# A recommendation-model kernel: the TensorE order around the pair products, and the output layers in three parts

## What is computed

```python
B, NF, D, V, NDENSE = (512, 26, 64, 12500, 13)      # as run
h = relu(dense @ dw1 + db1)
dense_emb = relu(h @ dw2 + db2)
sparse_emb = emb_tables[f_ids, sparse_idx]          # 512 x 26 rows of 64 floats
emb = concatenate([dense_emb[:, None, :], sparse_emb], axis=1)
inter = einsum('bfd,bgd->bfg', emb, emb)
pairs = inter[:, iu0, iu1]                          # 351 pairs
z = concatenate([emb.reshape(B, -1), pairs], axis=1)
z = relu(z @ ow1 + ob1)                             # 512 wide
z = relu(z @ ow2 + ob2)                             # 256
z = relu(z @ ow3 + ob3)                             # 128
return z @ ow4 + ob4
```

## Time and profile before

| | us |
|---|---|
| median of 3 runs | 188.66 |
| lowest and highest | 187.30, 188.84 |
| the profiled execution, its own time | 187.21 |
| its span (first to last instruction) | 185.4 |
| PE busy | 127.4 |
| POOL busy | 123.8 |
| mean granted TensorE clock | 0.88 of full |

### The profile page before, as it was taken

One profiled execution on the slowest core, in us unless ns is written; L12 is line 12 of the kernel. 1 busy time (PEld: TensorE's weight loads), 2 busy tenths in 40 slices (PEclk: granted clock), 3 DMA queues, 4 the chain that ended last, 5 costly groups with the idle time before them and its releaser, 6 DMA issues.

```text
span 185.4 us, 3069 instructions
## 1 busy us (share of the span) xinstructions
PE 127.4 (69%) x1301; PEld 68.8 (37%) x1301; DVE 37.8 (20%) x97; ACT 42.2 (23%) x96; POOL 123.8 (67%) x199
## 2 busy tenths in 40 slices
PE   1510285828655995839439993959729979989994
PEld 0000132514344442524226432424426446656453
DVE  2700003000142204100144005000234023136011
ACT  0440310031046201040075001040174011166011
POOL 3888888888735888888565888888367887200000
PEclk9999999975965699996965798587997999999999
DMA  5999532221212332312312332222222324100000
GB/s 157 409 332 357 172 26 23 23 28 21 21 13 23 21 22 24 28 22 26 24 13 24 23 27 20 23 28 20 19 20 20 22 25 31 18 4 0 4 0 0
DMA packets 4576, 9.80 MB, mean 53 GB/s; under 512 B 2065, under 2 KB 2065, under 8 KB 3922
## 3 DMA queue, kind: packets, MB, share of 16 engines
q0 software_dynamic: 3328, 3.41, 21.3%
q1 hardware_dynamic: 1010, 5.30, 7.1%
q10 hardware_dynamic: 224, 0.89, 1.6%
HBM read 9.59 MB, written 0.00 MB: 52 GB/s over the span
## 4 chain that ended last, share of the span: by engine, by line
PE 45%; POOL 26%; issue 18%; ACT 5%; DMA 3%; DVE 2%
PE acc L259 20%; POOL gathered L211 20%; PE acc L292 10%; PE inter L276 7%; POOL pace L219 6%; PE acc L310 4%; DMA gathered<-tables,rows 2%; ACT emb L386 1%; ACT emb L387 1%; PE turned L240 1%; PE acc L301 1%; ACT pairs L392 1%; DMA idx_raw<-idx 1%; ACT z L399 1%; DVE emb L466 1%
## 5 line engine op out<-in xcount | busy, mean ns | idle before, releaser
L211 POOL DMA_INDIRECT gathered<-tables,rows x104 | 98.9, 951 | 34.6 <-issue 16.9
L259 PE MATMUL acc<-w,emb 128*128 128x512 f32 x104 | 65.7, 780 | 19.4 <-issue 12.3
L259 PEld LDWEIGHTS acc<-w,emb 128*128 128x128 f32 x104 | 31.3, 315 | 46.3 <-issue 36.9
L392 ACT ACTIVATE pairs<-inter 28x96 f32<-28x96 f32 (+1 forms) x64 | 15.7, 246 | 39.8 <-PE inter L276 39.1
L219 POOL MEMSET pace<- 128x192 uint8 x90 | 24.7, 274 | 0.1
L292 PE MATMUL acc<-w,pairs 128*128 128x512 f32 x56 | 24.7, 592 | 0.0
L182 DVE COPY pairs<-inter 28x96 f32<-28x96 f32 (+1 forms) x64 | 17.0, 266 | 26.5 <-PE inter L276 25.8
L276 PE MATMUL inter<-emb 64*28 64x28 f32 x1024 | 12.6, 204 | 13.8 <-DMA gathered<-tables,rows 10.1
L240 PE MATMUL turned<-small,gathered 128*128 128x128 f32 x52 | 10.1, 317 | 13.5 <-DMA gathered<-tables,rows 13.5
L386 ACT ACTIVATE emb<-turned 128x512 f32<-128x512 f32 x8 | 8.8, 1098 | 45.7 <-issue 28.6
L465 DVE COPY emb<-turned 128x512 f32<-128x512 f32 (+1 forms) x7 | 5.5, 784 | 64.1 <-issue 49.5
(11 more groups left out here) (47 smaller groups left out, 26.3 us busy)
## 6 DMA issues: line engine op xcount, KB each, us to landing
w<-w SPq DMA_DIRECT2D x5, 1024.0 KB, 8.7
gathered<-tables,rows POOLq DMA_INDIRECT x104, 3.4
small<-small_pack ACTq DMA_DIRECT2D x1, 706.5 KB, 6.0
dense_sb<-dense_pack ACTq DMA_DIRECT2D x1, 160.5 KB
idx_raw<-idx SPq DMA_DIRECT2D x1, 39.0 KB
idx_raw<-idx SPq DMA_DIRECT2D x1, 13.0 KB, 1.9
out<-y SPq DMA_DIRECT2D x1, 2.0 KB
```

The source lines that it names most:

```text
L211: pool.indirect_dma_start(out=gathered[:, t, s, :], out_offset=None, in_=tables, in_offset=bass.IndirectOffsetOnAxis(ap=rows[:, t, s:s + 1 ...
L259: nc.tensor.matmul(acc[t][:], emb[:, tile_of(t), place(2 * c)], w[:, c, :], start=(c == 0), stop=False)
L392: last = move(lambda dst, src: nc.scalar.activation(dst, src, ACT.Copy), t, k, (0, 1))
```

## The change

Three things are moved on PE; ACT and DVE follow in their own orders. POOL's and SP's instructions are the same, but for the semaphores of the last tile's groups.

1. **The end of a tile.** Before, PE did `turn` 2, the four chunks of group 2, `turn` 3, the chunk of group 3, and then the first half-stage. Now it does `turn` 2, `turn` 3, the first two chunks of group 2, the first half-stage, `turn(t+1, 0)`, then the other two chunks of group 2 and the chunk of group 3, and only then the second half-stage.
2. **The output layers in three parts** (`PARTS`): tiles 0 and 1 together (256 columns) in tile 2; tile 2 (128 columns) with its layer 2 in tile 3 and its layers 3 and 4 beside the interactions of tile 3; tile 3 as before.
3. **The last tile has five groups**: 4, 4, 2, 2 and 1 chunks (`LAST_GROUPS`).

```diff
+LAST_GROUPS = [(0, 4), (4, 8), (8, 10), (10, 12), (12, 13)]
-EARLY = LAST * P
+PARTS = [slice(0, 2 * P), slice(2 * P, 3 * P), slice(3 * P, B)]
 ...
+def groups(t):
+    return LAST_GROUPS if t == LAST else GROUPS
 ...
-            def field_products(t, g, chunks=None):
+            def field_products(t, g, first=0, end=W_GROUP):
 ...
-                for c in range(*(chunks or GROUPS[g])):
+                c0, c1 = groups(t)[g]
+                for c in range(c0 + first, min(c0 + end, c1)):
 ...
             for t in range(TILES):
                 if t:
                     interactions(t - 1, 0)
                 turn(t, 0)
                 if t:
+                    field_products(t - 1, 2, 2)
+                    field_products(t - 1, 3)
                     interactions(t - 1, 1)
                 field_products(t, 0)
                 if t:
                     pair_product(t - 1)
                     z1_to_features(t - 1, at_once)
                 turn(t, 1)
-                if t < LAST:
+                if t == LAST:
+                    break
+                if t == LAST - 1:
+                    layer2(PARTS[0], 1, whole, (acc[0], acc[1]))
+                    field_products(t, 1, 0, 2)
+                    layer3(PARTS[0], 0, acc[3])
+                    field_products(t, 1, 2)
+                    layer4(PARTS[0], 0, acc[0])
+                else:
                     field_products(t, 1)
-                    turn(t, 2)
-                    field_products(t, 2)
-                    turn(t, 3)
-                    field_products(t, 3)
-
-            layer2(early, LAST - 1, [[(m, k) for m in range(2) for k in range(K1)]], (acc[0], acc[1]))
-            c0, c1 = GROUPS[1]
-            field_products(LAST, 1, (c0, c0 + 1))
-            layer3(early, 0, acc[2])
-            field_products(LAST, 1, (c0 + 1, c0 + 3))
+                turn(t, 2)
+                turn(t, 3)
+                field_products(t, 2, 0, 2)
+
+            layer2(PARTS[1], 2, whole, (acc[1], acc[2]))
+            field_products(LAST, 1)
             turn(LAST, 2)
-            layer4(early, 0, acc[0])
-            field_products(LAST, 1, (c0 + 3, c1))
             turn(LAST, 3)
-            c0, c1 = GROUPS[2]
+            field_products(LAST, 2)
+            turn(LAST, 4)
             interactions(LAST, 0)
-            field_products(LAST, 2, (c0, c0 + 2))
+            layer3(PARTS[1], 1, acc[1])
+            field_products(LAST, 3)
             interactions(LAST, 1)
-            field_products(LAST, 2, (c0 + 2, c1))
-            field_products(LAST, 3)
+            field_products(LAST, 4)
+            layer4(PARTS[1], 1, acc[2])
             pair_product(LAST)
             z1_to_features(LAST, Z1_STEPS)
-            layer2(late, LAST, LAYER2_STEPS, (acc[1], acc[2]))
-            layer3(late, 1, turned[1])
-            layer4(late, 1, inter[0])
+            pe.wait_ge(y_done, 2)
+            layer2(PARTS[2], LAST, LAYER2_STEPS, (acc[1], acc[2]))
+            layer3(PARTS[2], 2, turned[1])
+            layer4(PARTS[2], 2, inter[0])
```

More of the change, by code:

```diff
@@ L124, in build @@
         ones_set = sem("ones_set")
-        group_in = [[sem(f"group_in{t}_{g}") for g in range(NG)] for t in range(TILES)]
+        group_in = [[sem(f"group_in{t}_{g}") for g in range(len(groups(t)))] for t in range(TILES)]
         gathers_held = sem("gathers_held")
@@ L207, in _ @@
                     pool.wait_ge(rows_done, 1)
-                for g, (c0, c1) in enumerate(GROUPS):
+                for g, (c0, c1) in enumerate(groups(t)):
                     for s in range(2 * c0, 2 * c1):
@@ L231, in turn @@
             def turn(t, g):
-                c0, c1 = GROUPS[g]
+                c0, c1 = groups(t)[g]
                 pe.wait_ge(group_in[t][g], 2 * (c1 - c0) * 16)
@@ L241, in turn @@
                                              gathered[:, t, 2 * c:2 * c + 2, :].rearrange("p f d -> p (f d)"), ident)
-                if t == LAST and g == NG - 1:
+                if t == LAST and g == NG:
                     moved(t - 1)
@@ L248, in kept @@
             def kept(t, g):
-                pe.wait_ge(kept_dve if g % 2 else kept_act, t * 2 + g // 2 + 1)
-                if t == LAST and g == NG - 1:
-                    pe.wait_ge(kept_act, t * 2 + 3)
-            def field_products(t, g, chunks=None):
+                if g % 2 or g == NG:
+                    pe.wait_ge(kept_dve, t * 2 + g // 2 + 1)
+                if g % 2 == 0:
+                    pe.wait_ge(kept_act, t * 2 + g // 2 + 1)
+            def field_products(t, g, first=0, end=W_GROUP):
                 if t == 0:
@@ L266, in interactions @@
                         pe.wait_ge(dense_placed, 1)
-                    kept(t, 2)
-                    kept(t, 3)
+                    for g in range(2, len(groups(t))):
+                        kept(t, g)
                     if t:
@@ L326, in layer4 @@
                 nc.tensor.matmul(bank[0:1, 0:n], ow4, z3t[:, samples], start=True, stop=True).then_inc(y_mm, 1)
-            early, late = slice(0, EARLY), slice(EARLY, B)
             at_once = [(0, K1)]
+            whole = [[(m, k) for m in range(2) for k in range(K1)]]
             for t in range(TILES):
@@ L385, in keep @@
                 act.wait_ge(group_turned, t * NG + g + 1)
-                nc.scalar.activation(evens(t, g), turned_all(g), ACT.Copy)
-                nc.scalar.activation(odds(t, g), turned_odds(g), ACT.Copy).then_inc(kept_act, 1)
+                nc.scalar.activation(evens(t, g), turned_all(t, g), ACT.Copy)
+                nc.scalar.activation(odds(t, g), turned_odds(t, g), ACT.Copy).then_inc(kept_act, 1)
             def moves(t, k):
@@ L425, in _ @@
                     z1_relu(t - 1, at_once)
+                if t == LAST - 1:
+                    z2_relu(PARTS[0], 0, acc[0])
+                    z3_relu(PARTS[0], 0, acc[3])
                 if t == LAST:
-                    z2_relu(early, 0, acc[0])
-                    z3_relu(early, 0, acc[2])
+                    z2_relu(PARTS[1], 1, acc[1])
                 keep(t, 2)
-            act.wait_ge(group_turned, TILES * NG)
-            nc.scalar.activation(odds(LAST, NG - 1), inter[0][D:P, 0:P].rearrange("p (c b) -> p c b", b=P), ACT.Copy) \
+            act.wait_ge(group_turned, LAST * NG + NG + 1)
+            nc.scalar.activation(odds(LAST, NG), inter[0][D:P, 0:P].rearrange("p (c b) -> p c b", b=P), ACT.Copy) \
               .then_inc(kept_act, 1)
             moves(LAST, 0)
+            z3_relu(PARTS[1], 1, acc[1])
             moves(LAST, 1)
             z1_relu(LAST, Z1_STEPS)
-            z2_relu(late, 1, acc[1])
-            z3_relu(late, 1, turned[1])
+            z2_relu(PARTS[2], 2, acc[1])
+            z3_relu(PARTS[2], 2, turned[1])
         @block.vector
@@ L499, in _ @@
                 keep(t, 1)
+                if t == LAST - 1:
+                    z2_relu(PARTS[0], 0, acc[1])
+                    outputs(PARTS[0], 0, acc[0])
                 if t == LAST:
[L501 to L506, removed]
+                    z2_relu(PARTS[1], 1, acc[2])
+                keep(t, 3)
+            dve.wait_ge(group_turned, LAST * NG + NG + 1)
+            nc.vector.tensor_copy(evens(LAST, NG), turned_all(LAST, NG)).then_inc(kept_dve, 1)
             moves(LAST, 0)
             moves(LAST, 1)
+            outputs(PARTS[1], 1, acc[2])
             z1_features(LAST, Z1_STEPS)
-            z2_relu(late, 1, acc[2])
-            outputs(late, 1, inter[0])
+            z2_relu(PARTS[2], 2, acc[2])
+            outputs(PARTS[2], 2, inter[0])
 def lay_out(inputs):
```

23 lines of the change are left out of this document (10 added, 13 removed).

## The result

| | before | changed |
|---|---|---|
| median, us | 188.50 | 195.20 |
| lowest and highest, us | 187.30, 188.84 | 193.27, 196.36 |
| span of the profiled execution, us | 185.4 | 194.5 |

The changed kernel is slower: 1.029 times the time before, 95% interval 1.022 to 1.036. That ratio compares executions in the faster of two states that a kernel shows, of the changed kernel those of 193.27 and 194.11 us; its two others, the profiled one among them, took 196.3 and 196.4 us and lift its median to 195.20. The forecast was no change at 189.4 us, from 185.9 to 192.4; the time lies above that.

The account below looks back on a forecast made before the run. POOL was taken to set the pace up to tile 3's second held gather, PE the end. 187.21 us plus 2.9 (holds), 0 (layers) and -1.2 (tail) gave 188.9, with 0.5 added 189.4 us; range 185.9 to 192.4.

Parts of the forecast that it names:

- The hold term: POOL, gather 7 to gather 11 in tiles 1 to 3: 10.7 us each, +2.9 us in all, from -3.1 to +5.0.
- may go after the longer wait: First half-stage: its inner stall of 0.82 us may vanish, which moves little since the landing comes next.
- The mechanism of the holds: Around the half-stages: PE idles about 5 us ahead, its clock falls, and the six records behind take 4.5 us.
- the high end: Holds with all six records at 1.2 GHz: 11.4 us a pair, 34.2 us in all, +5.0 us.
- The rival with half clock at both places: Slow clock between the half-stages in all tiles and in the tail: +5.3, or 192.5 us; chance 0.31.
- The tail term: End of the last tile: last chunk turned earlier, shorter way to the pair product; -1.2 us, from -2.7 to +0.3.
- the +1.5 us: Tail: price for PE's clock falling after its new waits, taken between 0 and 3 us.
- The layers in tile 2: Layers of tiles 0 and 1 done in tile 2 fit into the room made: 0 us, from 0 to +3.
- tile 2 overfull: Layers at half clock make PE up to 3 us late at tile 2's first half-stage: 191 us and more; chance 0.06.
- The offset of 0.5 us: Added for the unchanged stretches: a third of the 1.45 us by which the timed median exceeds the profiled execution.

Follow-up runs that it names:

- changed_again: The changed kernel with no edit, run once more on another chip for a second profile; 1.031 times the time before.
- padded_12: The changed kernel with three idle 128x128 matmuls (12 records with weight loads) behind the two chunks ahead of each first half-stage; 1.022 times the time before.
- before_again: The kernel before with no edit, run once more on another chip for its time and profile; 1.001 times the time before.
- shifted_28: The changed kernel with seven idle 128x128 matmuls (28 records with weight loads) at the very start; 1.028 times the time before.
- products_before_turn3: The changed kernel with the two chunks of group 2 ahead of the transpose of group 3 instead of behind it; 1.033 times the time before.
- two_between: The changed kernel with two chunks instead of three between the half-stages and three ahead of the first; 1.004 times the time before.
- layers_only: The kernel before with only the output layers in three parts, old order around the half-stages, four groups in the last tile; 1.001 times the time before.
- holds_undone: The changed kernel with all five field products of a tile's end ahead of the first half-stage again; 0.990 times the time before.

## Why the prediction was wrong

**The hold term failed, and by its size.** The step "three times 10.7 is 32.1: +2.9 us" measured +5.1 us on the first chip, for which it was made (34.24 against 29.16), and +8.3 us on the others (34.2 against 25.9).
- The end it named, 10.7 us a pair, is right where the half-stage runs through: 10.52 and 10.62 us in tiles 1 and 3 of changed_again, 10.40 to 10.60 in padded_12. The six records took 4.35, 5.11 and 4.91 us where 4.5 stood.
- The stop in tile 1's half-stage was put at nothing: such stalls "may go after the longer wait", and "that moves little". On the first chip they came to 0.71 and 1.37 us there and the pair of tile 2 to 12.86 us, 2.2 us over 10.7. That is the whole miss of the term on that chip (34.24 - 32.1 = 2.1). In changed_again one stop of 2.59 us brings 13.06 us.
- The base depends on the chip. The kernel before has 29.16 us there and 25.9 in before_again. The earlier trace rows show a part of the difference: tile 1's first half-stage stops for 0.82 us inside (tile 0's, in the same trace, for 0.59 and 0.52), and in before_again it does not. The three timed executions on the first chip were no shorter than the profiled one, so nothing shows that these stalls were a chance of one execution. Whether they are that chip's is open. Against the other chips' base the term was 5.4 us short: 3.3 for the base, 2.6 for the stop, and 0.5 the other way, since the pairs without the stop come to 31.6 instead of 32.1.

**That leaves a part of the miss on the first chip.** The two quicker executions lie 3.9 and 4.7 us above the forecast, and the holds explain 2.2. If their last gather starts where the profiled one's does, their tails are 28.4 and 29.2 us (an estimate: spans of 191.5 and 192.3 us, less 163.1) against 27.2 before, +1.2 and +2.0 us where -1.2 stood. No profile of such an execution exists there, so the cause of this part is open.

**The mechanism of the holds was right.** PE's wait of 4.8 to 6.5 us ahead of the half-stages in changed_again, the clock at 0.50 behind it, and the chunks ending after gather 10 are all there; what the earlier trace rows showed of eight records held for six. That the +5.1 us of the first chip meet the high end I had given (+5.0) is luck: that end had three slow pairs of 11.4 us and no stop, and it was reached by 10.57, 10.81 and one pair of 12.86 with the stop. The rival with half clock at both places (192.5 us, 0.31) was the nearest case. Its 11.4 us a pair was too high: the six records ran at 0.50 nearly to their end, but the half-stage behind them had the full clock and took 1.27 instead of 1.75 us.

**The tail term, -1.2 us, measured -2.0 in changed_again, and other profiles put it nearer zero.** In changed_again the last chunk is turned at 166.50, 3.45 us after its gather starts, instead of 5.8 us: -2.4 against -2.2 expected. From turn to half-stage +0.2, from half-stage to pair product 175.09 - 167.74 = 7.35 us against 7.3, where 7.1 against 7.6 stood: the narrow end gains nothing there, because the moves lie open (0.94 us). The clock stayed at 1.00, and the +1.5 us for a fallen one did not come. But in padded_12, shifted_28, products_before_turn3 and two_between, whose tile 3 is the same, it did: the four records between the half-stages took 2.9 to 3.6 us instead of 1.99, and the tail is 26.7 to 27.0 us, only 0.2 to 0.5 under that of before_again. In padded_12, with the granted clock in the window:

```profile
167.05 3.52 PE L266 MATMUL acc<-w,emb 128*128 128x512 f32 x4
```

```profile
168.00:169.00 1.00, 1.00 (x3) 0.50 0.00 0
```

And in changed_again:

```profile
169.47 1.99 PE L266 MATMUL acc<-w,emb 128*128 128x512 f32 x4
```

PE's waits before it are nearly the same in two_between, where the clock fell (1.55, 0.33 and 0.80 us), and in changed_again, where it did not (1.53, 0.34 and 0.80). So the +1.5 us, a middle between 0 and 3, was a fair price for something that came in some profiles and not in others; what decides it is open.

**The layers in tile 2, 0 us, held.** In changed_again PE waits 6.51 us ahead of tile 2's first half-stage. The rival "tile 2 overfull" did not happen. With all five chunks ahead of it the same layers do no sure harm either: the pair of tile 3 is 8.52 us in layers_only, and in holds_undone, the same kernel up to there, 9.53.

**The offset of 0.5 us** rested on the profiled execution being quick among its neighbours. No run prices it. What the other chips add is where the chips differ: spans of 185.4 and 182.2 us, 3.2 apart, and pairs of 29.16 and 25.91 us, 3.25 apart.

## What to carry to other kernels

Work moved into a wait must fit into it at the lower clock if PE has idled before: here one chunk (1.9 us) fits, two cost 1.3 to 1.4 us in tiles 1 and 2 and three 1.6 to 2.1 us a tile, on the engine that sets the pace. When two holds of the pacing engine hang on another engine, whatever of the work between them is longer than the wait there is on the critical path. Before a difference is priced, stalls in the base want a price of their own, in the kernel before and in the changed one. And one profile gives a stretch one value: the same tile 3 took 25.2 or 27.0 us here.

## What was not expected of the hardware

- PE can stop inside a burst of small matmuls, here for 2.3 to 2.9 us, and a 16 KB transfer on the instruction queue falls into the stop. That it is PE's instruction supply is read from that and from the place: it moved from 120 to 107 records when 28 instructions were inserted far ahead. With 12 cheap instructions more, of under 1 us, ahead of each first half-stage it was gone. With three to five chunks ahead of the half-stage, or two and idle matmuls, the transfer before it fell between 73 and 82 us; with two chunks alone there was none until 93 to 94. What makes PE ask for it is open.
- In the first profile of the changed kernel PE's signals reached ACT and DVE up to 3.8 us after the end that the trace gives for the transpose (turned at 162.0 to 162.4, copy at 166.15), and 2.2 us after it in tile 2 (turned by 124.0, copy at 126.25). The kernel before, on the same chip, shows 0.75 us of it once, between layer 3 (done at 159.89) and its relu (160.64). It did not come again in fourteen later profiles on other chips, and its cause is open.
- The same kernel, the one before, took 188.5 us on the first chip and 184.1 to 184.6 on the others, with the ratio of the change the same (1.029 and 1.031).
